# Where the expert weights are cut into two halves: two pieces in the prologue, two per step of the attention loop, the last expert's four behind the last tile

## The reference

```python
x = x + xattn(layernorm(x), ctx, ctx, abundance, ...)        # 16 heads, 64 keys, log(abundance) added to the scores
scores = softmax(layernorm(x) @ gate_w.T)
sel = top_k(scores + expert_bias, 2)
routed = layernorm(x)[token_idx] * top_scores_sorted         # tokens sorted by expert
h = silu(routed_e @ w1[e]) * (routed_e @ w3[e])              # hidden width 704
out = out + h @ w2[e]                                        # summed back per token
x = x + out
```

## Time and profile before

| | |
|---|---|
| median of 3 runs | 461.13 us (460.94 to 462.37) |
| profiled execution | 461.81 us, span 460.1 us |
| mean granted TensorE clock | 0.888 of 2.4 GHz |
| busy share: PE, DVE, ACT, POOL | 80%, 56%, 42%, 50% |

### The profile page before, as it was taken

How to read it: one execution, slowest core, us unless ns; L and a number is a source line. 1 busy time by engine, 2 the same in 40 slices (tenths; PEclk the granted TensorE clock), 3 DMA queues, 4 the chain that set the end, 5 groups by cost and what they waited for, 6 DMA issues and landing times.

```text
span 460.1 us, 10326 instructions
## 1 busy us (share of the span) xinstructions
PE 368.7 (80%) x2657; PEld 271.7 (59%) x2658; DVE 258.0 (56%) x635; ACT 195.2 (42%) x351; POOL 232.2 (50%) x281
## 2 busy tenths in 40 slices
PE   2765998999999774011899999999999999999830
PEld 1533777777877663010567677767777776777620
DVE  2775666767666216984455555555555555556400
ACT  2155686757576444400334343333443344333300
POOL 6367547443445535803235555655565556565340
PEclk9865999999999665555999999999999999999985
DMA  5904253323336262302367777777777777788636
GB/s 152 351 23 139 59 206 110 119 77 125 108 120 195 73 213 68 103 0 49 79 131 131 133 134 132 132 136 138 138 139 135 136 134 136 133 135 133 98 56 194
DMA packets 106677, 57.55 MB, mean 125 GB/s; under 512 B 82581, under 2 KB 101282, under 8 KB 106626
## 3 DMA queue, kind: packets, MB, share of 16 engines
q1 hardware_dynamic: 98848, 46.78, 40.4%
q0 software_dynamic: 7488, 10.39, 15.4%
q10 hardware_dynamic: 322, 0.15, 0.1%
HBM read 28.62 MB, written 11.60 MB: 87 GB/s over the span
## 4 chain that ended last, share of the span: by engine, by line
PE 70%; DVE 11%; DMA 5%; issue 5%; POOL 3%; ACT 2%; POOLq 0%; SPq 0%; DVEq 0%; ACTq 0%
PE sc L1353 11%; PE sc L1355 10%; PE sc L1354 10%; PE bank L1238 5%; PE bank L1369 5%; PE bank L1372 5%; PE bank L1371 4%; PE bank L1307 3%; PE ptps L1283 3%; POOL w_lo L526 2%; DMA acc<-xn,put_now 2%; PE bank L1296 2%; DMA w_hi<-n_L_xattn_in_proj_weight 1%; PE sc L1162 1%; DVE arena L850 1%
## 5 line engine op out<-in xcount | busy, mean ns | idle before, releaser
L1353 PE MATMUL sc<-w_hi,arena 128*128 x312 | 98.5, 316 | 12.2 <-DMA arena<-xn 8.9
L1354 PE MATMUL sc<-w_hi,arena 128*128 x312 | 98.1, 315 | 0.0
L1355 PE MATMUL sc<-w_lo,arena 128*128 x312 | 98.1, 314 | 0.0
L609 POOL DMA_INDIRECT acc<-xn,put_now x39 | 62.5, 1601 | 70.5 <-DVE xn L1121 58.5
L526 POOL TENSOR_TENSOR w_lo<-stage_w,w_hi 128x1408 f16<-128x1408 f32 (+3 forms) x32 | 71.8, 2256 | 45.7 <-ACT w_hi L633 45.0
L1108 DVE SCALAR_TENSOR_TENSOR arena<-sc,slot_score,arena 128x352 f32<-128x352 f32 x78 | 45.5, 584 | 85.1 <-ACT arena L778 83.8
L778 ACT ACTIVATE arena<-sc,slot_score 128x352 f32<-128x352 f32 x78 | 43.1, 553 | 116.9 <-PE sc L1355 116.9
L1369 PE MATMUL bank<-w_hi,arena 128*128 x234 | 63.8, 273 | 3.3 <-DVE xn L1121 1.8
L1372 PE MATMUL bank<-w_lo,arena 128*128 x234 | 61.7, 273 | 0.0
L578 POOL DMA_INDIRECT arena<-table,get_now x39 | 42.4, 1086 | 33.3 <-POOL get_now L575 31.4
L1371 PE MATMUL bank<-w_hi,arena 128*128 x195 | 53.2, 273 | 0.0
(11 more groups left out here) (191 smaller groups left out, 638.3 us busy)
## 6 DMA issues: line engine op xcount, KB each, us to landing
stage_w<-in_L_ffn_w SPq DMA_DIRECT2D x16, 704.0 KB, 4.2
stage_w<-in_L_ffn_w SPq DMA_DIRECT2D x16, 256.0 KB, 2.9
stage_w<-in_L_ffn_w SPq DMA_DIRECT2D x32, 64.0 KB, 2.7
acc<-arena SPq DMA_DIRECT2D x16, 128.0 KB, 1.7
table<-xn SPq DMA_DIRECT2D x16, 128.0 KB, 1.8
arena<-in_x SPq DMA_DIRECT2D x2, 896.0 KB, 6.3
arena<-table,get_now POOLq DMA_INDIRECT x39
arena<-xn SPq DMA_TRANSPOSE x39
```

Source lines behind the costliest of these rows:

```text
L609: pool.indirect_dma_start(out=acc[:, :], out_offset=bass.IndirectOffsetOnAxis(ap=put_now[par][:, 0:1], axis=0), in_=y_sb[par], in_offset=N ...
L1353: pe.matmul(ps[:, c, :], gT[par][:, k, :], w_hi[:, cols], start=k == 0, stop=False)
L1354: pe.matmul(ps[:, c, :], gT[par][:, KD + k, :], w_hi[:, cols], start=False, stop=False)
L1355: ins = pe.matmul(ps[:, c, :], gT[par][:, k, :], w_lo[:, cols], start=False, stop=k == KD - 1)
```

## The change

The pieces are dealt out anew. Two pieces of expert 0 are loaded ahead of the bulk of x and split in the middle of the prologue; the other two stay where they were. Steps 0 and 1 have no piece, steps 2 to 5 one each, steps 6 to 15 two each (the second at the end of the step on ScalarE, directly behind the first on GpSimd), steps 16 to 19 none of the early experts' pieces. The four pieces of expert 7 come in steps 17 and 18 on ScalarE; on GpSimd the first comes in step 17 and three behind step 19. From step 16 on ScalarE does the copy `oT` first in its step. Beside that, an exponential on one column is done in the prologue, so that its table is loaded there; the statistics of later tiles and the split of the output bias move to the end of VectorE's steps 0 and 1; and the projection of the keys is computed on 128 columns and spread by the copy out of PSUM (256 columns before).

```diff
-        STEP_HALVES = [(1, 0), (1, 1), (2, 1)] + [(e, 0) for e in range(2, 7)] + [(3, 1), (4, 1)]
-        BESIDE = {4: (5, 1), 14: (6, 1)}
...
+        for t in range(2, T):
+            if t < 6:
+                piece_at(t, 1, (t - 2) // 2, t % 2, 0)
+            else:
+                piece_at(t, t // 2 - 1, 0, t % 2, 0)
+                piece_at(t, t // 2 - 1, 1, 1 - t % 2, 1)
         LATE = len(PIECES)
-        PIECES += [(E - 1, g, kind, 1 - g) for g in range(2) for kind in range(2)]
+        PIECES += [(E - 1, g, kind, g) for g, kind in ((0, 0), (1, 1), (0, 1), (1, 0))]
...
-            for n in range(AHEAD):
+            for n in range(2):
+                load(n)
+            for b in range(B):
+                load_rest_of_x(b)
+            for n in range(2, AHEAD):
                 load(n)
...
                 if t is None:
-                    load(loop_piece(u, par) + 1, 1 - par, u + par - 1)
...
+                    n = loop_piece(u, par)
+                    load(n + 2, 1 - par, u + par - 1, 0, n)
+                    load(n + 3, par, u + par - 1, 1, n)
...
+            for n in range(2):
+                piece_low(n)
+
             pool.wait_ge(s["bias_parts"], 1)
...
                 if t is None:
                     weights_low(loop_piece(u, par), stage[par][0], loop_columns(u, par))
+                    weights_low(loop_piece(u, par) + 1, stage[1 - par][1], loop_columns_beside(u, par))
...
+                if t == T + 1:
+                    pool.wait_ge(s["o_ps"], T)
+                    piece_low(LATE)
...
             tokens_high(0)
+            piece_high(0)
...
+            piece_high(1)
...
+                if t is None:
+                    weights_high(loop_columns_beside(u, par), rank(at_step[6][1])[0] + u - 3, 1 - par, 1)
+                else:
+                    for n in at_step[t][1:]:
                         piece_high(n)
+                if t == T + 1:
+                    act.wait_ge(s["pt_ps"], 2 * T)
+                if t in (T + 1, T + 2):
+                    for n in range(2):
+                        piece_high(LATE + 2 * (t - T - 1) + n)
...
-                dve.tensor_scalar(kT[:, c].rearrange("p b r s -> p (b r s)"), sc_ps[1][:, c * 512:c * 512 + B * P],
-                                  bias_qk[:, 2 + c:3 + c], HD ** -0.5, ALU.add, ALU.mult).then_inc(s["kT_sb"], 1)
+                dve.tensor_scalar(kT[:, c], sc_ps[1][:, c * 512:c * 512 + B * S2].rearrange("p (b s) -> p b s", b=B)
+                                  [:, :, None, :].broadcast_to([P, B, 2, S2]), bias_qk[:, 2 + c:3 + c], HD ** -0.5, ALU.add, ALU.mult).then_inc(s["kT_sb"], 1)
```

More of the change, by code:

```diff
@@ L331, in _, with load_rest_of_x, load @@
             sp.wait_ge(s["wkv_load"], 16)
-            for b in range(B):
+            def load_rest_of_x(b):
                 sp.dma_start(xs[:, b + 2:T:2, :], x[b, P:N, :].rearrange("(u p) d -> p u d", p=P))\
                     .then_inc(s[f"x_load{b}"], 16)
-            def load(n, kind=None, expert=None):
+            def load(n, kind=None, expert=None, half=0, freed=None):
                 if kind is None:
@@ L346, in load @@
                 else:
-                    e, g, buf = bass.ds(expert, 1), 0, 0
-                    sp.wait_ge(s["whi"], n - 1)
-                    sp.wait_ge(s["wlo"], n - 1)
+                    e, g, buf = bass.ds(expert, 1), half, half
+                    sp.wait_ge(s["whi"], freed)
+                    sp.wait_ge(s["wlo"], freed)
                 dst, loaded = stage[kind][buf], w_loads[kind][buf]
@@ L371, in _ @@
             sp.dma_start(acc[TOK:TOK + P, :], zero_rows).then_inc(s["zero_st"], 16)
-            load(AHEAD)
+            for n in (AHEAD, AHEAD + 1):
+                load(n)
             def step(u, par, t):
                 if t is None:
-                    load(loop_piece(u, par) + 1, 1 - par, u + par - 1)
-                if t == T - 2:
-                    load(at_step[t][1])
-                if t is not None and t + 1 < STEPS:
+                    n = loop_piece(u, par)
+                    load(n + 2, 1 - par, u + par - 1, 0, n)
+                    load(n + 3, par, u + par - 1, 1, n)
+                elif 2 <= t < T - 1:
                     for n in at_step[t + 1]:
[L382 to L385, removed]
+                        if n >= AHEAD + 2:
+                            load(n)
+                elif t in (T - 1, T):
+                    for n in range(2):
+                        load(LATE + 2 * (t - T + 1) + n)
                 if here(t, 2):
@@ L514, in _ @@
             assert n_c[0] == N_CONST
[L517 to L520, removed]
-                                   key_diag[:, None, :].broadcast_to([P, H, S2]), ALU.mult).then_inc(s["beta_s"], 1)
             def weights_low(number, staged, cols):
@@ L530, in piece_low @@
                 weights_low(n, stage[kind][buf], piece_columns(n))
+            for n in range(2):
+                piece_low(n)
+            pool.wait_ge(s["bias_parts"], 1)
+            for b in range(B):
+                pool.tensor_tensor(beta[:, b, :].rearrange("p (h s) -> p h s", h=H),
+                                   bias16[:, b * H:(b + 1) * H, None].broadcast_to([P, H, S2]),
+                                   key_diag[:, None, :].broadcast_to([P, H, S2]), ALU.mult).then_inc(s["beta_s"], 1)
             first_scales(*LN_GROUPS[1], 2)
             pool.wait_ge(s["kb_dve"], 8)
-            for n in range(AHEAD):
+            for n in range(2, AHEAD):
                 piece_low(n)
@@ L711, in step @@
                     ln1(t, tt + 2, par)
+                if t is not None and t >= T:
+                    outputs_across(t, tt)
                 if here(t, 3):
@@ L992, in step @@
                     queries_low(tt + 1, 1 - par)
+                if t in (0, 1):
+                    for n in range(6 + 5 * t, 11 + 5 * t):
+                        first_stats(n)
+                if t == 1:
+                    first_moments(*LN_GROUPS[2])
+                if t == 1:
+                    dve.wait_ge(s["bo_load"], 16)
+                    link(dve.tensor_copy(bo16[:, :], bo_all))
+                    link(dve.scalar_tensor_tensor(out=bo_rest, in0=bo16[:, :], scalar=low_rows[:, 0:1], in1=bo_all,
+                                                  op0=ALU.mult, op1=ALU.add))
+                    dve.tensor_copy(bo16[:, :], bo_rest).then_inc(s["bo_s"], 1)
                 if t == T + 3:
```

62 lines of the change are left out of this document (22 added, 40 removed).

## The result

| | before | after |
|---|---|---|
| median | 461.03 us | 457.01 us |
| single runs | 460.69 to 462.37 (4) | 454.68, 455.26, 458.77, 461.62 |
| mean granted clock of these runs | 0.888 (profiled) | 0.914, 0.915, 0.899, 0.892 |

The ratio is 0.988, with a 95% interval from 0.984 to 0.992: faster by 1.2%, which is clear of no change but under 2%. It leaves out the run of 461.62, which lies over 1.5% above the fastest. The two medians of four runs are 4.0 us apart. The forecast was 454.3. The four runs after the change differ by 6.9 us, and their time goes with the clock. The profiled execution is the one of 461.62 (span 459.8); it is read here for where the time lies, and its one fall of the clock in the loop is told apart.

A forecast was written before the change was run, and what follows sets the result against it. TensorE was taken as nearly full except in two half-clock holes (slices 2 to 4, 13 to 18), routing's end set by GpSimd's last pieces. Terms -3.6 + 5.0 - 8.2 = -6.8 us off 461.13 gave 454.3 us, range 449 to 462.5.

The forecast's parts named there:

- the signs that it named: Prologue, even steps, selection: queries about 22, no load wait, xn2T waits 1.0 to 1.5 us, selection some 42 behind step 15.
- a sign of being wrong: Loop: a granted clock of 0.5 between 75 and 145 us would show that TensorE's clock falls there.
- the sum (-6.8): Whole kernel: -3.6 + 5.0 - 8.2 = -6.8 us, taken off the median 461.13.
- Prologue and steps 0 to 2: From the start through step 2: -1.2 - 3.4 + 1.0 = -3.6 us; bounds about -8 and -0.5.
- The lock: Prologue: two GpSimd pieces hold up VectorE's four key-spreading operations by 4.5 us, or 2.9 by the beta rows.
- the statistics: Steps 0 to 2: moved to VectorE's step ends, they bring step 2 3.4 us sooner and cost about 1.0 at its head.
- Rival 1: Prologue: VectorE is not locked; about 4 us more gain, 450 us; chance 0.16.
- Steps 3 to 15: Attention loop: -1.3 + 5.1 + 1.2 = +5.0 us; bounds +2.5 and +6.5.
- the charge for a two-piece step: Loop: 1.27 us each for steps 8, 10, 12, 14 (+5.1); 0.3 each for steps 7, 9, 11, 13 (+1.2).
- Rival 2: Loop: TensorE's clock falls, 4.5 us each; one fall 458.8 (chance 0.12), two 463.3 (two or more 0.13).
- Step 15 to the selection: End of attention and routing: 41.5 us instead of 49.7, -8.2 us; bounds -11 and -4.
- Rival 3: Routing end not freed: last pieces still lock VectorE's last operations; last term -4, 458.5 us; chance 0.09.

The follow-up runs named there:

- experiment 2: Changed kernel, but from step 6 GpSimd forms a step's second low half behind the next step's normalisation instead of ahead of it; 443.62 us, ratio 0.960.
- the sixth experiment: Changed kernel, but second pieces of steps 14 and 15 go behind the last tile, five pieces instead of three behind the last normalisation; 455.96 us, single run.
- experiment 9: Changed kernel, but TensorE makes twelve unread transposes in even steps 6 to 14 where it would stand for xn2T; 454.86 us, ratio 0.985.
- Experiments 4: Changed kernel, but statistics of later tiles and the output bias split stand ahead again in VectorE's steps 0 and 1; 458.28 us, one run.
- fifth: Changed kernel, but ScalarE copies the outputs (oT) ahead of its first rounding in every step; 457.24 us, ratio 0.989.

## Why the prediction was right, and where not

Most of the signs that it named came: two pieces between the spreads and the first queries at 21.39 (forecast 22.2), no wait for a load at `queries_high(1)`, waits for `xn2T` in even steps (1.64 us, forecast 1.0 to 1.5), and the selection 41.7 us behind step 15 (forecast 41.5). Two did not: step 15 started 7.3 us later than before, not 1, and the clock was at 0.50 from 94.5 us on, which was a sign of being wrong. That the sum (-6.8) came close to the 4.0 us between the medians is in part luck: two of its terms were off in opposite directions, by -1.9 and, without the fall of the clock, by +3.9.

**Prologue and steps 0 to 2: mis-sized, -5.5 where -3.6 stood.** The mechanism was right. The lock took 4.1 us (forecast 4.5, bounds 0 and 4.5 with 2.9 by the beta rows), and the statistics gave at most 3.15 and took back 1.10. What was too small was the gain around them: the loads landed 0.65 earlier in this execution, and step 1, forecast at 37.3, began at 35.93, at full clock. TensorE's idle time ahead of the queries, said to be 6 us more than before, was 6.03 in all, 4.1 more. Chance is as large as the error: three traces with the same code up to there (experiments 2, 6 and 9) have step 3 at 45.55, 47.77 and 48.22, which would make the term -5.8 to -8.5. Rival 1 (no lock) did not happen. With the lock removed step 3 came 6 us earlier in one pair of traces; some 4 of that are the lock, the rest is the clock. The lock did not always fall on the spreads: in the sixth experiment's trace the two pieces ran first, from 12.68 for 4.49 us, and the spreads took 2.48, but the cast and the subtraction ahead of them took 2.96 and 1.74 us instead of 0.29 and 0.43, and the first queries came at 21.02, where the other traces with the early pieces have 20.67 to 21.39.

The Trainium skill (SBUF — State Buffer, Who interferes with whom) says that a VectorE instruction with two SBUF inputs and a GpSimd instruction that reads SBUF lock each other out. The traces agree here: 6.58 us beside two pieces, 2.49 us without, and 3.00 us beside a late piece again.

**Steps 3 to 15: the step that failed is the charge for a two-piece step.** 1.27 for an even step and 0.3 for an odd one were taken from step 5 of before and from a guess at TensorE's slack. Measured, without the fall, even steps 10, 12 and 14 are 1.7 to 2.0 longer than before and odd ones 0.7. The wait is 1.64, not 1.27, a second one of 0.43 for `oT` stands behind it, and an odd step waits 0.43. Moreover step 5 of before, with its wait of 1.27, was 1.55 longer than step 5 after the change, so that the wait alone was too small a charge even there. By experiment 9, which has no fall, the term is +8.9 (100.39 - 91.51), beyond the upper bound of +6.5; its unread work lengthens step 6 by 0.74, and step 7 is as much shorter. Experiments 4 and 6 (101.33 and 101.43) come to the same without their falls of about 1 us each. The sum of the steps agrees: the even ones cost 7.6 and not 5.1, the odd ones 2.9 and not 1.2, and step 5 gave 1.55. The cause was named rightly: with the second piece behind the normalisation the loop is at 89.93, below before's 91.51. So all of the loop's loss was the order on GpSimd, not the second piece as such.

**Rival 2, the fall of the clock, was given too little.** In the profiled execution it fell once, in step 8, for 10 us, and cost 3.9 (104.32 against experiment 9's 100.39; step 8 took 11.20 and step 9 10.66, where 9.79 and 7.97 are usual); forecast 4.5. In experiments 4 and 6 a fall cost about 1. The run of 458.77 fits one fall by its time and its mean clock, 0.899, but has no trace. With a fall in each of five traces, 0.25 for one fall or more was too low. The comparison with stalls of 3.06 and 2.29 us left out a shorter one in the same rows: TensorE stood 1.93 us at 18.64, and its clock was 0.50 from 20 to 25 us.

**Step 15 to the selection: right, -8.0 for -8.2, with two errors that cancel.** The last normalisation ended 32.1 us behind step 15's start, not 30.9, and from there the selection took 9.5, not 10.6. Three pieces were left behind the last normalisation, and routing was 7.1 us shorter from there. Five pieces lengthen it by 4.3. Rival 3 did not happen.

What stays open: which even step makes the clock fall in an execution, and for how long (steps 8 and 12 have the same two waits; three traces lost it in step 8, two in step 12), and some 2.5 us between the two fastest runs (454.68, 455.26) and the profiled one less its fall (457.7). A prologue that happened to be faster, as in experiment 2, could account for these, but there is no trace of those runs.

## What to carry to other kernels

Work that is put on a helper engine costs by what stands behind it there: in this kernel the same two pieces per step lost 8.9 us where the second stood ahead of a small operation that TensorE waits for, and nothing where it stood behind it. Before splitting a wait into many short ones, look at what the clock does behind each: in this kernel a stall of 2 us cost another 1 to 3.9 when the clock fell. And when two kernels' loops differ, compare the stage behind them too: in one pair of traces here a gain of 3.3 us in the loop was lost again behind it, because the clock fell there in one execution and not in the other.

## What was not expected of the hardware

The changed kernel and five of the experiments (the second, fourth, fifth, sixth and ninth, in this order) have the same code up to step 0, and yet step 0 begins at 29.62, 26.59, 28.90, 27.76, 27.03 and 27.64 us. Loads that land up to 0.7 us apart are a part of it; the greater part is the clock behind an idle time of 5.2 to 6.0 us (in the sixth experiment 4.2 and 1.1). Experiment 2, then the changed kernel:

```profile
24.00:28.00 4.00, 4.00 (x18) 2.12 (x17) 4.00 (x6) 2.19 (x9) 1.94 (x1) 1.00 0.06 18
```

```profile
24.00:28.00 4.00, 4.00 (x10) 2.24 (x8) 4.00 (x4) 1.25 (x5) 2.38 (x2) 0.50 0.29 89
```

With 1.00 (2.4 GHz) TensorE does 18 matmuls in these 4 us, with 0.50 (1.2 GHz) 10. Step 1 shows the same: where VectorE has the changed order it takes 4.74 or 4.75 us in five traces (clock 1.00), and 6.40 in the other five (clocks of 0.57 to 0.64). So when single runs of this prologue are compared, up to 3 us are chance.
